# Layer 1: the low part of the row maxima made by TensorE and copied out by ScalarE

## The chip, the cores and the metric

The kernel runs on one core of one Trainium2 chip. The metric is the device time of one execution in microseconds (us). Three runs of the kernel before gave 2096.59, 2102.5 and 2103.61 us; the median is 2102.5 us.

## What is computed

The reference is two transformer layers over x of shape (64, 64, 256), each a cross attention and a mixture of experts:

```
x = x + L0_xattn(layernorm(x), ctx)        # 8 heads of 8 channels, 256 positions, rotary
x = x + L0_ffn(layernorm(x))               # 64 experts, 8 chosen, no capacity
x = x + L1_xattn(layernorm(x), ctx)        # as above, biases on q, k, v, no rotary, no output matrix
x = x + L1_ffn(layernorm(x))               # 64 experts, 8 chosen, capacity 128 each
```

In an attention, scores = q k / sqrt(8), p = softmax(scores), out = p v. For the change only one detail matters. The softmax subtracts the maximum of each row of scores. The kernel does this inside the product: q gets extra rows that hold minus the row maximum, and k has ones there. The products are in bf16, so the maximum is given in two bf16 rows, a high part (the maximum rounded to bf16) and a low part (what the rounding left).

## The kernel before, in words

Both layers have an attention stage and an expert stage, with barriers between them. The attention stage of a layer goes over 32 pairs of batches as a pipeline written out by hand. A pair passes the stages load, comb, front, stack, smax, attn, back, route, place and post, one stage in each step, so a step works on up to ten pairs at once. A step has 16 units u = 0..15. In each engine's program one function `body(st)` lists, unit by unit, what that engine does in the step; engines work their lists in order and meet only at semaphores.

Abbreviations used below, for unit u of a step:

- S(u): TensorE makes scores of the smax pair (line 1534) into one of three banks psS. VectorE then takes the row maxima from it (line 1145, "reduction"), negated, into mx. S(u) waits for the reduction of u-3.
- T(u): TensorE makes the transposed scores of the attn pair (line 1547), two matmuls, into one of two banks psE; ScalarE takes the exponential of it (line 943, "exp(u)"). T(u) waits for exp(u-2).
- values: TensorE multiplies four exponentials with v (line 1570, 16 matmul records) at u = 2 (for the pair in stage back), 7, 11 and 15.
- V: TensorE's product of the context with the value matrix (line 1618, recorded under 1585), at u = 4 in layer 1. Its bank is psO, and it waits until ScalarE has copied the attention output out of that bank at u = 3 (line 923, osb).
- RK: two small products for the routing ranks at u = 2 (line 1608); LIST: eight products for the token lists at u = 14 (line 1656), after ScalarE has copied out the router's logits at u = 13.

The row maxima of a pair come in two halves, h = 0 and h = 1. For each half the order of work is: TensorE transposes 16 columns of mx into a small bank (items mT1 at u = 1 for the attn pair, mT0 at u = 10 for the smax pair); ScalarE copies the bank to bf16, the high part mhi (`max_rows`, line 930); VectorE subtracts the high part from the bank, the low part mlo (`split_max`, line 1152), at u = 2 for h = 1 and at u = 11 for h = 0; the sync engine's queue writes both into rows of q2 (lines 674 and 706). T(0) waits for the half h = 0 of its pair, T(8) for h = 1. The small bank comes free for the next item when the low part is done (semaphore s_mlo).

In layer 1 ScalarE also multiplies gathered expert rows at u = 0..3 (line 950), normalises at u = 4 and 6 (lines 991 and 983), and TensorE's Q product at u = 7 waits for the second of these. POOL gathers those rows with eight indirect DMAs a step, paced by the exponentials.

Of the kernel before, what the change touches and what calls it, by code (L numbers as in the profile page):

```python
# [28 lines left out]
ALU = mybir.AluOpType  # L29
# [173 lines left out]
def build(nc, x, ctx, tables, wts, out):  # L203
    stack = ExitStack()
    with stack:
        def sb(name, shape, dt=F32):
            return stack.enter_context(nc.sbuf_tensor(name, shape, dt))

        def sem(name):
            return stack.enter_context(nc.semaphore(name))  # L210

        def sems(name, n=NB):
            return [sem(f"{name}{i}") for i in range(n)]
# [19 lines left out]

        ident = sb("ident", [P, P])
        ones = sb("ones", [P, P], BF16)
        tri = sb("tri", [P, P], BF16)
        tri0 = sb("tri0", [P, P], BF16)
        iota_e = sb("iota_e", [P, E])
# [148 lines left out]
        s_p1, s_rem, s_p2, s_p3 = (sem(n) for n in ("s_p1", "s_rem", "s_p2", "s_p3"))  # L387
        s_score, s_max = sem("s_score"), sem("s_max")
        s_mhi, s_mT, s_mlo = sems("s_mhi", 2), sems("s_mT", 2), sems("s_mlo", 2)
        s_st, s_exp = sem("s_st"), sem("s_exp")  # L390
        s_pv, s_oev = sem("s_pv"), sem("s_oev")
        s_vp, s_v = sem("s_vp"), sem("s_v")
# [514 lines left out]
        def _(act):  # L907
# [5 lines left out]
            def body(st):  # L913
# [11 lines left out]
                def max_rows(stage, h):  # L925
                    act.wait_ge(s_mT[h], st.n(stage))
                    before = Step(L, st.s0 - 1, st.it)
                    if before.s0 >= LAG[stage]:
                        act.wait_ge(d_max[h][before.buf(stage)], before.nbuf(stage, 32))
                    a.copy(mhi[h][:, :], small[item_bank(L, f"mT{h}")][0:16, 0:P]).then_inc(s_mhi[h], 1)  # L930

                filled = L == 1 and st.s0 == FULL - 2
                for u in range(UNITS):
                    if u == 15 and 0 <= st.s0 - AHEAD < EARLY // 2:
# [40 lines left out]
                        a.copy(xT[:, :, :].rearrange("p c t -> p (c t)"), small[item_bank(L, "XT")][:, 0:2 * P]).then_inc(s_xT, 1)  # L975
                    if u == 10 and st.on("smax"):
                        max_rows("smax", 0)
                    if u == (14 if filled else 4) and (st.on("front") or st.on("route")):
                        act.wait_ge(s_rstd, 4 * st.roots())
                    if u == (14 if filled else (4, 6)[L]) and st.on("front"):  # L980
# [79 lines left out]
        def _(dve):  # L1060
# [54 lines left out]
            for b in range(NB):  # L1115
                for o in range(2):
                    v_.memset(ones_of(b, o), 1.0)
            v_.tensor_copy(iota_e[:, :], iota_i[:, 0:E])
            v_.scalar_tensor_tensor(tri0[:, :], ident[:, :], CHOSEN, tri[:, :], ALU.mult, ALU.add)
            v_.tensor_copy(slotk[:, :], slot_i[:, :])  # L1120
            v_.tensor_copy(base0[:, :], base_i[:, :])
# [16 lines left out]
            def body(st):  # L1138
# [10 lines left out]
                def split_max(stage, h):  # L1149

                    dve.wait_ge(s_mhi[h], st.n(stage))
                    v_.tensor_tensor(mlo[h][:, :], small[item_bank(L, f"mT{h}")][0:16, 0:P], mhi[h][:, :], ALU.subtract)\
                      .then_inc(s_mlo[h], 1)
# [75 lines left out]
                for u in range(UNITS):  # L1229
# [21 lines left out]
                    if L == 1 and u == 9 and st.on("back"):  # L1251
# [3 lines left out]
                        wait(dve, d_x1[b], lastbuf(st, "back"))  # L1255
                        v_.scalar_tensor_tensor(x1[b][:, :], small[item_bank(1, "NT")][:, 0:T], bias[:, 8:9],
                                                xres[b][:, :], ALU.add, ALU.add).then_inc(s_x1, 1)
                    if u == 11 and st.on("smax") and not filled:
                        split_max("smax", 0)
                    if u == 1 and st.on("post") and L == 1:  # L1260
                        ch.join("ranks")
# [9 lines left out]
                    if L == 1 and st.s0 >= FULL - 1:  # L1271
                        sums(st, u)
                    if filled and u == 7:
                        split_max("smax", 0)
                        sums(Step(1, FULL - 3), 0)
                    if L == 1 and st.s0 < FULL - 1 and st.s0 != FULL - 3 and u == 15:
                        sums(st, 0)
# [29 lines left out]
                    if u == 0 and st.on("post") and L == 1:  # L1307
# [1 line left out]
                        wait(dve, s_lsp, st.n1("post", 1, 0))  # L1309
                        v_.tensor_tensor(twos(hotr[:, :, :]), over_k(rank_at), in_twos(0, P), ALU.is_equal)\  # L1310
                          .then_inc(s_lhs, 1)
                    if u == 2 and st.on("attn"):
                        split_max("attn", 1)
                    if L == 0 and u == 12 and st.on("back"):
                        b = st.buf("back")
# [205 lines left out]
        def _(pe):  # L1521
# [3 lines left out]
            def body(st):  # L1525
# [49 lines left out]
                def product(item, stage, ready, terms, done, n=T):  # L1575

                    for semaphore, value in ready:
                        pe.wait_ge(semaphore, value)
                    ps = psE[0] if item == "Q" and L == 1 and st.s0 == FULL - 2 else bank(pe, st, item)
                    for i, (lhs, rhs) in enumerate(terms):  # L1580
                        if rhs is None:
                            w = lhs.shape[1] if len(lhs.shape) == 2 else 32
                            ins = m_.transpose(ps[0:w, i * P:(i + 1) * P], lhs, ident[:, :])
                        else:
                            ins = m_.matmul(ps[:, i * n:(i + 1) * n], lhs, rhs, start=True, stop=True)
                    ins.then_inc(done, 1)

                def rows_of_x(st):
                    b = st.buf("route")
                    product("XT", "route", [(s_xr, st.n("route"))],  # L1590
                            [(xr[b][:, i * P:(i + 1) * P], None) for i in range(2)], s_xtp)

                def q_rows(st):
                    b = st.buf("front")
                    product("Q", "front", [(s_xn, st.n("front"))],
                            [(wbd[L][n][:, :], xn[b][:, :]) for n in ("qr", "q")[L]], s_qp)

                for u in range(UNITS):
# [2 lines left out]
                    if st.on("attn"):  # L1601
                        scores_t(u)
                    if u == 1 and st.on("attn"):
                        product("mT1", "attn", [(s_max, st.n("attn", UNITS))],
                                [(mx[st.buf("attn")][:, 1, :], None)], s_mT[1])
                    if u == 2 and st.on("place"):
                        b = st.buf("place")
                        product("RK", "place", [(s_mask, st.n("place"))],
# [26 lines left out]
                        product("NT", "back", [(s_nrm, st.n("back"))],  # L1635
                                [(nrm[:, h, :], None) for h in range(2)], s_ntp)
                    if u == 10 and st.on("smax"):
                        product("mT0", "smax", [(s_max, st.n("smax", UNITS, 8))],
                                [(mx[st.buf("smax")][:, 0, :], None)], s_mT[0])
                    if L == 0 and u == 10 and st.on("route"):  # L1640
                        rows_of_x(st)
                    if u == 12 and st.on("back") and L == 0:
# [137 lines left out]
```

## Time and profile before

| what | value |
|---|---|
| median of three runs | 2102.5 us |
| the profiled execution | 2111.01 us |
| its span (first to last instruction) | 2109.3 us |
| mean granted TensorE clock | 0.940 |
| busy share of the span: TensorE matmul, weight load | 79%, 52% |
| busy share: VectorE, ScalarE, GpSimd | 66%, 59%, 46% |

Matmuls overlap in TensorE's pipeline and their ends are modelled, so its busy share says little by itself. The page's list of costliest groups is headed by the reductions (681.1 us in 1024 instructions) and the exponentials (599.6 us in 1024, with 324.1 us of idle ScalarE time ahead of them, 263.2 us of it ended by a matmul of T). Those groups hold both layers. The attention stage of layer 1 is the stretch of some 675 us that ends with the reductions and exponentials at about 1844 us. In a timeline row the columns are: start in us, duration in us (of a merged row from its first start to its last end), engine, line, operation, output and inputs, size, count; in brackets the idle time of the engine before it and what ended that.

### The profile page before, as it was taken

Reading aid. Unit: us, or ns where it says so; the run is one execution under the profiler, and the core shown is the slowest. Engines: PE = TensorE matmul, PEld = TensorE weight load, DVE = VectorE, ACT = ScalarE, POOL = GpSimd, SP = SyncE. Lnnn points to the kernel's source line nnn. Section 1 sums busy time; section 2 is a strip of 40 time slices with the busy share of each in tenths; the row PEclk is TensorE's granted clock in tenths of the full one; section 3 lists DMA queues with packets and bytes.
Section 4 is the critical chain, followed back from the end, with each engine's and each line's share of the span. In section 5 each row is a group of like instructions: output and inputs, shape, how many; then the busy total and the mean of one; then the engine's idle time right before and its main releaser. Section 6 shows DMA issues by size and latency. Waiting matters only on the chain. (4 is left out here: it accounts for less than half of the span.)

```text
span 2109.3 us, 44138 instructions
## 1 busy us (share of the span) xinstructions
PE 1657.1 (79%) x12469; PEld 1104.4 (52%) x12623; DVE 1387.0 (66%) x4213; ACT 1238.4 (59%) x3174; POOL 978.2 (46%) x1114
## 2 busy tenths in 40 slices
PE   3999999999855999999994577777777778856651
PEld 2555555555534898899883244444444434444431
DVE  5888888888844455554334678878888778743331
ACT  1777777777642566666663467767777767722110
POOL 4277777777662000000004655555555553148883
PEclk9999999999987999999996799999999999968896
DMA  5688877777746966666664768877677676268856
GB/s 144 159 232 237 225 210 206 212 209 205 195 145 221 290 204 196 203 195 203 198 190 144 187 173 210 205 193 179 175 176 183 160 178 155 72 170 186 184 94 111
DMA packets 413082, 390.90 MB, mean 185 GB/s; under 512 B 46640, under 2 KB 385072, under 8 KB 412848
## 3 DMA queue, kind: packets, MB, share of 16 engines
q1 hardware_dynamic: 346496, 265.28, 47.1%
q0 software_dynamic: 37904, 90.22, 16.8%
q10 hardware_dynamic: 28448, 32.59, 5.5%
q8 instruction: 110, 1.80, 0.4%
q14 instruction: 124, 1.02, 0.2%
HBM read 233.74 MB, written 170.16 MB: 191 GB/s over the span
## 5 line engine op out<-in xcount | busy, mean ns | idle before, releaser
L1145 DVE TENSOR_REDUCE mx<-psS 128x2 f32<-128x512 f32 x1024 | 681.1, 682 | 176.9 <-PE psS L1534 113.4
L943 ACT ACTIVATE prob<-psE 128x512 f32<-128x512 f32 x1024 | 599.6, 600 | 324.1 <-PE psE L1547 263.2
L792 POOL DMA_INDIRECT yg<-y_d,row_all x256 | 252.4, 986 | 676.1 <-SPq L418 478.9
L1547 PE MATMUL psE<-q,k 128*128 128x256 bf16 x2048 | 397.3, 276 | 88.3 <-ACT prob L943 55.0
L1534 PE MATMUL psS<-k,q 128*128 128x512 bf16 x870 | 338.6, 390 | 27.3 <-DVE mx L1145 13.5
L1673 PE MATMUL psE<-wt,xgT 128*128 (+1 forms) x1536 | 327.2, 337 | 1.0 <-ACT xgT L1039 0.4
L779 POOL DMA_INDIRECT xs_d<-xr,row_all x256 | 252.0, 984 | 144.3 <-ACT prob L943 97.4
L1547 PEld LDWEIGHTS psE<-q,k 128*128 128x128 bf16 x2048 | 183.4, 99 | 254.6 <-ACT prob L943 119.0
L1486 DVE TENSOR_TENSOR hid<-sil,psE 128x96 f32<-128x96 f32 x384 | 97.7, 254 | 329.8 <-ACT sil L1044 307.0
L1570 PE MATMUL psO<-prob,v 128*32 128x256 f32 x4096 | 282.3, 394 | 0.0
L1039 ACT COPY xgT<-psS 128x256 f32<-128x256 f32 x384 | 144.5, 376 | 184.7 <-PE psS L1667 119.2
L1673 PEld LDWEIGHTS psE<-wt,xgT 128*128 128x128 f32 x1536 | 249.1, 196 | 6.3 <-issue 4.8
L1685 PE MATMUL psM<-wt,hT 96*128 (+1 forms) x768 | 235.1, 388 | 0.0
L1667 PE MATMUL psS<-ident,xg 128*128 128x128 f32 x768 | 155.0, 284 | 93.1 <-DMA xg<-xn_d,idx 82.0
L1667 PEld LDWEIGHTS psS<-ident,xg 128*128 128x128 f32 x768 | 105.0, 145 | 154.0 <-DMA xg<-xn_d,idx 87.0
L1534 PEld LDWEIGHTS psS<-k,q 128*128 128x128 bf16 x1024 | 103.1, 101 | 155.1 <-issue 76.0
L1048 ACT COPY y_all<-psM 128x256 f32<-128x256 f32 x320 | 119.2, 373 | 87.7 <-PE psM L1685 87.4
L1570 PEld LDWEIGHTS psO<-prob,v 128*32 128x32 f32 x4096 | 108.6, 111 | 96.7 <-issue 41.6
L1044 ACT ACTIVATE sil<-psE 128x96 f32<-128x96 f32 x384 | 96.6, 252 | 96.0 <-PE psE L1673 90.6
L1685 PEld LDWEIGHTS psM<-wt,hT 96*128 96x128 f32 x768 | 118.9, 195 | 15.5 <-issue 0.4
L838 POOL TENSOR_TENSOR parts<-rem,parts 128x512 bf16<-128x512 f32 x64 | 74.1, 1158 | 68.7 <-ACT parts L1017 33.3
L830 POOL TENSOR_TENSOR rem<-qk,parts 128x512 f32<-128x512 f32 x64 | 74.2, 1160 | 37.1 <-ACT parts L1008 22.9
(226 smaller groups left out, 2446.3 us busy)
## 6 DMA issues: line engine op xcount, KB each, us to landing
xg<-xs_d SPq DMA_DIRECT2D x320, 128.0 KB, 2.6
y_d<-y_all SPq DMA_DIRECT2D x320, 128.0 KB, 2.3
q<-q_stack_d SPq DMA_DIRECT2D x128, 256.0 KB
k<-k_stack_d SPq DMA_DIRECT2D x128, 256.0 KB
wt<-in_gu ACTq DMA_DIRECT2D x110, 192.0 KB
q_stack_d<-parts SPq DMA_DIRECT2D x64, 192.0 KB
k_stack_d<-parts SPq DMA_DIRECT2D x64, 192.0 KB
wt<-in_dn ACTq DMA_DIRECT2D x110, 96.0 KB
```

The costliest lines, as they stand in the source:

```text
L779: g.indirect_dma_start(xs_d[:, :], bass.IndirectOffsetOnAxis(row_all[:, row(st.pair(stage) * K + k, 1)], 0), xr[b][:, 0:T], None).then_inc ...
L792: g.indirect_dma_start(yg[:, k, :], None, y0_d[:, :], bass.IndirectOffsetOnAxis(row_all[:, row(st.pair("load") * K + k, 1)], 0))\
L943: a.activation(prob[gr][:, u % 4, :], psE[ring][:, :], ACT.Exp, scale=SCALE).then_inc(s_exp, 1)
L1039: a.copy(xgT[st.buf("X", 2)][:, :, :].rearrange("p c t -> p (c t)"), psS[st.buf("X", 2)][:, 0:2 * P]).then_inc(s_xgT, 1)
L1048: a.copy(y[st.buf("D")], psM[st.buf("D", 2)][:, 0:T]).then_inc(s_y, 1)
L1145: v_.tensor_reduce(mx[b][:, bg // 4, :].rearrange("p (h r) -> p h r", h=2)[:, :, (bg % 4) * 2 + tt], psS[(UNITS * (st.s0 - LAG["smax"]) + ...
L1534: m_.matmul(psS[(UNITS * (st.s0 - LAG["smax"]) + u) % 3][:, :], q2[b][:, bg, tt * P:(tt + 1) * P], k2[b][:, bg, :], start=True, stop=True) ...
L1547: ins = m_.matmul(psE[ring][:, i * T:(i + 1) * T], k2[b][:, bg, hh * T + i * P:hh * T + (i + 1) * P], q2[b][:, bg, :], start=True, stop=True)
L1570: ins = m_.matmul(psO[32 * j:32 * j + 32, half * T:(half + 1) * T], v[b][:, i, unit_at(4 * q + j), :], prob[gr][:, j, i * T:(i + 1) * T], ...
L1667: ins = m_.transpose(psS[i][:, c * P:(c + 1) * P], xg[b][:, c * P:(c + 1) * P], ident[:, :])
L1673: ins = m_.matmul(psE[i][:, 0:2 * I], xgT[i][:, c, :], weights_of(st, "GU", table, P, 2 * I * c, 2 * I), start=(c == 0), stop=(c == 1))
L1685: m_.matmul(psM[i][:, 0:T], hT[i][:, :], weights_of(st, "D", table, I, 4 * I, T), start=True, stop=True).then_inc(s_yp, 1)
```

## The change

In layer 1 VectorE no longer makes the low part; layer 0 keeps it. A new tile `minus` holds minus the identity, 16 by 16, in bf16. In layer 1 TensorE, one unit after the transposition (u = 2 for h = 1, u = 11 for h = 0), waits until the high part is made, and then writes the same 16 by 128 place of the small bank again with two matmuls: the maxima times the identity in f32, and, added to it, minus the identity times the high part. ScalarE copies the sum out as the low part at u = 3 (h = 1) and u = 12 (h = 0). The DMAs that carry the parts, and the semaphore that frees the bank, stay.

```
+        minus = sb("minus", [16, 16], BF16)
+        s_rest = sems("s_rest", 2)
 # ScalarE
+                def max_rest(stage, h):
+                    act.wait_ge(s_rest[h], st.n1(stage))
+                    a.copy(mlo[h][:, :], small[item_bank(L, f"mT{h}")][0:16, 0:P]).then_inc(s_mlo[h], 1)
...
+                    if L == 1 and u == 3 and st.on("attn"):
+                        max_rest("attn", 1)
+                    if L == 1 and u == 12 and st.on("smax"):
+                        max_rest("smax", 0)
 # VectorE
+            v_.tensor_scalar(minus[:, :], ident[0:16, 0:16], -1.0, None, ALU.mult)
...
-                    if u == 11 and st.on("smax") and not filled:
+                    if L == 0 and u == 11 and st.on("smax"):
                         split_max("smax", 0)
...
-                        split_max("smax", 0)
...
-                    if u == 2 and st.on("attn"):
+                    if L == 0 and u == 2 and st.on("attn"):
                         split_max("attn", 1)
 # TensorE
+                def less_high(stage, h):
+                    pe.wait_ge(s_mhi[h], st.n(stage))
+                    rest = small[item_bank(L, f"mT{h}")][0:16, 0:P]
+                    m_.matmul(rest, mx[st.buf(stage)][:, h, :], ident[:, :], start=True, stop=False)
+                    m_.matmul(rest, minus[:, :], mhi[h][:, :], start=False, stop=True).then_inc(s_rest[h], 1)
...
+                    if L == 1 and u == 2 and st.on("attn"):
+                        less_high("attn", 1)
...
+                    if L == 1 and u == 11 and st.on("smax"):
+                        less_high("smax", 0)
```

On TensorE the new pair at u = 2 stands after T(2) and before RK and the values of u = 2; at u = 11 it stands after T(11) and the values of u = 11, and before S(12). On ScalarE the new copy at u = 3 stands after exp(3), a product of the gathered rows and the copy osb, and before exp(4); at u = 12 after exp(12) and osb, and before exp(13).

## Rows read from the trace of the kernel before

**Rows 1.** Busy time and instructions by stretch; last: clock, DMA share, GB/s.

```profile
core 0: us, PE busy (x) PEld busy (x) DVE busy (x) ACT busy (x) POOL busy (x), PEclk, DMA share, GB/s
1169.00:1843.90 674.90, 517.26 (x4456) 283.03 (x4535) 555.12 (x1437) 477.93 (x1116) 354.15 (x428) 0.96 0.69 173
...
1506.50:1514.52 8.02, 6.00 (x51) 3.82 (x50) 7.28 (x20) 7.93 (x20) 3.85 (x4) 1.00 0.43 123
1514.52:1527.25 12.73, 9.54 (x91) 5.11 (x94) 10.26 (x30) 7.46 (x17) 7.05 (x10) 1.00 0.82 186
...
1502.50:1505.90 3.40, 3.40 (x28) 1.45 (x26) 1.73 (x9) 1.28 (x3) 2.54 (x5) 0.50 0.56 169
```

**Rows 2.** Groups by line and shape, 1250 to 1760: busy, mean ns, idle before.

```profile
L1152 DVE TENSOR_TENSOR mlo<-psM,mhi 16x128 bf16<-16x128 f32 x48 | 12.9, 269 | 0.8 <-ACT mhi L930 0.6 <-issue 0.2
...
L943 ACT ACTIVATE prob<-psE 128x512 f32<-128x512 f32 x385 | 228.4, 601 | 138.4 <-PE psE L1547 115.6 <-remote 18.5 <-PE psO L1570 2.4
...
L1585 PE MATMUL psO<-proj_v,ctx 128*128 128x128 f32 x96 | 16.4, 293 | 37.7 <-ACT osb L923 22.0 <-issue 15.7
```

**Rows 3.** Timeline of ScalarE in the first units of one step.

```profile
1506.50 0.60 ACT L943 ACTIVATE prob<-psE 128x512 f32<-128x512 f32 x1 [1.81 <-PE psE L1547]
...
1508.27 0.24 ACT L930 CAST mhi<-psM 16x128 bf16<-16x128 f32 x1
1508.41 0.58 ACT L943 ACTIVATE prob<-psE 128x512 f32<-128x512 f32 x1
...
1509.77 0.58 ACT L943 ACTIVATE prob<-psE 128x512 f32<-128x512 f32 x1
...
1510.65 0.36 ACT L923 COPY osb<-psO 128x256 f32<-128x256 f32 x1
1510.90 0.61 ACT L943 ACTIVATE prob<-psE 128x512 f32<-128x512 f32 x1
...
1512.31 0.60 ACT L943 ACTIVATE prob<-psE 128x512 f32<-128x512 f32 x1
```

**Rows 4.** Timeline of TensorE in the same units.

```profile
1507.15 0.39 PE L1547 MATMUL psE<-q,k 128*128 128x256 bf16 x2
1507.38 0.19 PE L1585 MATMUL psM<-mask,tri 128*128 128x64 bf16 x1
...
1508.76 0.38 PE L1547 MATMUL psE<-q,k 128*128 128x256 bf16 x2 [0.16 <-issue]
...
1511.15 0.68 PE L1585 MATMUL psO<-proj_v,ctx 128*128 128x128 f32 x4 [1.57 <-ACT osb L923]
1511.67 0.38 PE L1534 MATMUL psS<-k,q 128*128 128x512 bf16 x1
1511.89 0.38 PE L1547 MATMUL psE<-q,k 128*128 128x256 bf16 x2
```

**Rows 5.** Timeline of VectorE in the same units.

```profile
1509.02 0.27 DVE L1152 TENSOR_TENSOR mlo<-psM,mhi 16x128 bf16<-16x128 f32 x1
1509.22 0.67 DVE L1145 TENSOR_REDUCE mx<-psS 128x2 f32<-128x512 f32 x1
...
1512.09 0.69 DVE L1145 TENSOR_REDUCE mx<-psS 128x2 f32<-128x512 f32 x1 [0.74 <-PE psS L1534]
```

**Rows 6.** Timeline of TensorE from unit 11 to the next step.

```profile
1520.35 1.07 PE L1570 MATMUL psO<-prob,v 128*32 128x256 f32 x16
...
1524.63 0.61 PE L1657 MATMUL psM<-hote,hotr 128*128 128x128 bf16 x8 [0.57 <-ACT logit L1013]
1525.07 0.38 PE L1534 MATMUL psS<-k,q 128*128 128x512 bf16 x1
...
1526.83 0.38 PE L1547 MATMUL psE<-q,k 128*128 128x256 bf16 x2 [0.16 <-issue]
```

**Rows 7.** Timeline of ScalarE at units 10 and 12 of that step.

```profile
1521.42 0.24 ACT L930 CAST mhi<-psM 16x128 bf16<-16x128 f32 x1
...
1523.02 0.60 ACT L943 ACTIVATE prob<-psE 128x512 f32<-128x512 f32 x1 [0.87 <-PE psE L1547]
```

**Rows 8.** Timeline of the sync engine's queue in that step.

```profile
1523.10 0.54 SPq L706 DMA_DIRECT2D q<-mlo  x1
```

More of the change, by code:

```diff
@@ L1591, in rows_of_x, with max_columns @@
                             [(xr[b][:, i * P:(i + 1) * P], None) for i in range(2)], s_xtp)
+                def max_columns(stage, h, units):
+                    product(f"mT{h}", stage, [(s_max, st.n(stage, UNITS, units))], [(mx[st.buf(stage)][:, h, :], None)],
+                            s_mT[h])
+                def less_high(stage, h):
[3 more added lines that the diff above has]
+                    m_.matmul(rest, minus[:, :], mhi[h][:, :], start=False, stop=True).then_inc(s_rest[h], 1)
                 def q_rows(st):
@@ L1603, in body @@
                     if u == 1 and st.on("attn"):
-                        product("mT1", "attn", [(s_max, st.n("attn", UNITS))],
-                                [(mx[st.buf("attn")][:, 1, :], None)], s_mT[1])
+                        max_columns("attn", 1, UNITS)
+                    if L == 1 and u == 2 and st.on("attn"):
+                        less_high("attn", 1)
                     if u == 2 and st.on("place"):
@@ L1637, in body @@
                     if u == 10 and st.on("smax"):
-                        product("mT0", "smax", [(s_max, st.n("smax", UNITS, 8))],
-                                [(mx[st.buf("smax")][:, 0, :], None)], s_mT[0])
+                        max_columns("smax", 0, 8)
+                    if L == 1 and u == 11 and st.on("smax"):
+                        less_high("smax", 0)
                     if L == 0 and u == 10 and st.on("route"):
```

## The prediction

> **What bounds the kernel now.** The change touches only the attention stage of layer 1, so I read that stretch first and not the page's shares. By stretch, no engine is full over its 675 us: VectorE works 555 us, TensorE 517, ScalarE 478 [rows 1]. Such a stage is bound by a chain that runs from engine to engine, and the question is which engine holds it at the two places that change.
>
> The groups by line and shape tell how regular the stage is [rows 2]. In 510 us the low part is made 48 times, two a step, so there are 24 steps of about 21.2 us. Ahead of V TensorE was idle 37.7 us in 24 steps: 1.57 us each, ended by the copy osb, and the step that I follow has exactly 1.57 [rows 4]. So one step stands for the others.
>
> In that step the 8.02 us from exp(0) to the end of unit 6 have ScalarE busy 7.93 [rows 1]: up to there the chain runs on ScalarE. VectorE has 7.28 us in it and waits 0.74 us for S(5) [rows 5]. In the other 12.73 us ScalarE works only 7.46, and most of its 5.8 us of idle time a step (138.4 / 24) is ended by a T matmul [rows 1, 2]: there TensorE is late.
>
> So TensorE's position ahead of exp(3), and again ahead of exp(12), matters more than VectorE's work.
>
> **What is removed.** VectorE loses 0.269 us twice a step [rows 2]; from one start to the next it is 0.20 us [rows 5]. At u = 2 the next reduction would start 0.20 us earlier, but VectorE waits for S(5) two reductions later anyway, so this returns nothing. At u = 11 the reduction of u = 12 follows S(12), which, with T(12), stands behind the late values [rows 6, 7]. I take no gain; if VectorE did hold the chain it would be 64 x 0.20 = 12.8 us, and the few waits ahead of the subtraction (0.8 us) on top. That is one end of the range.
>
> **What is added at u = 2.** TensorE works in order, and now waits for the high part between T(2) and RK. T(2) starts at 1507.15 and RK at 1507.38 [rows 4]. The high part ends at 1508.27 + 0.24 = 1508.51, since ScalarE does it after exp(1) and a product of gathered rows [rows 3]. A release takes 0.05 us (exp(0) ends at 1507.10, T(2) starts at 1507.15). So the new pair starts at 1508.56.
>
> Its price is not in the trace. The nearest f32 matmul with 128 columns is V: two matmuls make four records, and from V to S(5) are 0.52 us, so one f32 matmul takes 0.26 [rows 4]. The bf16 one is bounded by LIST, eight of 128 columns in 0.44 us, 0.055 each [rows 6]. I take 0.32 together; the whole 0.68 us of V is the upper end, and 0.2 the lower.
>
> RK then starts at 1508.88, 1.50 us later. Queued behind are RK, the values of u = 2, S(3) and T(3). T(3) moves from 1508.76 to 1510.26. A T is ready for its exponential 0.42 us after its start (T(5) at 1511.89, exp(5) at 1512.31), so exp(3) starts at 1510.68 instead of 1509.77: 0.91 us late, because ScalarE was working on other things for the first 0.6 us of the delay.
>
> From exp(3) ScalarE keeps its own spacing: osb 0.88 us later (1511.56), the new copy at 1511.81, and exp(4) 0.14 us after that, the spacing of the high part's copy: 1511.95 instead of 1510.90, 1.05 late. V follows osb's end by 0.14 us, so it starts 0.91 us late, and with it S(5), T(5) and exp(5). ScalarE's own path to exp(5) has 1.05 at most. I take **0.91 us a step**; the cover of the new copy is V's wait, and without that cover it costs 0.14 more. VectorE's reductions from u = 3 on come as late, since S(3) stands behind the same wait. The work after unit 5 hangs on this chain (the second normalisation and Q), so nothing regular gives it back.
>
> **What is added at u = 11 and 12.** Here the pair stands behind the values of u = 11. The high part of this half ends at 1521.66 [rows 7], while the values start at 1520.35 and take 1.07 by the record [rows 6], and exp(12), which comes after them, starts at 1523.02 after 0.87 us of waiting for T(12). So the wait costs about nothing, but the pair's 0.32 us stand ahead of T(12), for which ScalarE waits: 0.32 on the path. The copy at u = 12 delays exp(13) and the logits by 0.14 us; LIST waits 0.57 us for the logits [rows 6], and S(15), T(15), the last values and the next T(0) stand behind LIST. So the 0.14 is on the path too: **0.46 us a step**. Lower end 0 (the late stretch swallows it), upper end 0.68 + 0.24.
>
> Of the moved copy the Trainium skill has a rule that speaks against it (ScalarE: Activation LUTs, Rules for kernel authors): multiplications, additions and the like belong on VectorE, which it gives as up to about three times faster. By that figure the copy would take an estimated 0.8 us, 0.57 more, and the sum would grow by 17 us in 30 steps. This trace does not agree for so small a tile: the copy of the same 16 by 128 takes 0.24 us on ScalarE [rows 3] and the subtraction 0.269 on VectorE [rows 2], and the sum goes by these.
>
> **The low part's way on.** The half h = 1 is written to q2 about 2 us later, long before T(8). The half h = 0 is needed by T(0) of the next step, at 1526.83 [rows 6]; the queue issued its low part at 1523.10 [rows 8]. It would be issued at about 1524.5, and T(0) itself comes 0.46 later, so some 2.8 us remain for a write of 4 KB. The issues queued behind it (x1 out, the next loads, the stack writes) move by up to 1.4 us, and what waits for them is over a unit away. I count nothing, and keep it as a rival. The small bank comes free later too, at u = 3 still ahead of K at u = 5, and K is behind V. The setup instruction and the new tile are single and cost nothing visible.
>
> **The sum.** 32 steps have the u = 2 pair; in the first the pipeline is still filling and I leave it out: 31 x 0.91 = 28.2 us. For u = 11 and 12 I count 30 of 32, since the last steps have no gathers and TensorE is less late: 30 x 0.46 = 13.8. Together 42.0 us on the profiled execution's 2111.0: 2153.0. The median of the runs is 8.5 us below that execution, so the forecast is 2102.5 + 42.0 = **2144.5 us**.
>
> **The rivals.**
>
> *A, the late stretch swallows the delay.* Between units 7 and 12 ScalarE waits for TensorE for longer than its recorded matmuls explain, in a stretch with a DMA share of 0.82 against 0.43 before it [rows 1]. If that ends by transfers that do not hang on the delayed chain, the 0.91 is lost in it, and 13.8 us stay: 2116.3; if it also swallows the pair of u = 11, nothing stays: 2102.5. Against it: those transfers are issued behind V, or paced by the exponentials, and so move with the chain.
>
> *B, VectorE holds the chain, and the kernel becomes faster.* VectorE is the busiest engine of the steps, 17.54 of 20.75 us [rows 1]. If TensorE's wait at u = 2 were covered by the 1.57 us that it waits ahead of V anyway, the relief of VectorE would count: 12.8 + 0.8 + some waits, about 15 us, 2087.5. It decides where exp(3) comes no later than now, that is where the delay of T(3) stays under 0.6 us instead of 1.50. Against it: the high part ends 1.36 us after T(2) starts, by two rows.
>
> *C, the clock.* After a pause TensorE's clock was granted at 0.50, the lower level of 1.2 GHz, from 1502.50 to 1505.90, and TensorE worked all of that time [rows 1]: at 2.4 GHz the same work takes half, so one such fall costs up to 1.70 us. The new wait makes another pause in each step. If each of the 23 regular steps fell once, 39 us come on top: 2183.5. Against it: the pause of 1.57 us ahead of V lies in a stretch granted at 1.00, and the new wait shortens it. The Trainium skill (TensorE: Matmul & The Clock Gate, HAM oscillation) says that waits between bursts of matmuls put the clock back to half; the trace agrees for the one fall shown, not for the pause ahead of V.
>
> *D, the low part lands late.* If its write takes 0.7 us longer than the 2.8 that remain, T(0) waits in 30 steps: 21 us more, 2165.5.
>
> **How the numbers follow.** Chances: forecast 0.60, A 0.15 (half of it at each of its two times), B 0.14, C 0.07, D 0.04. About 0.3%, 6 us, is what a measurement of this kernel can tell from no change. Faster by more: B, 0.14. Within: the lower half of A, 0.07. Slower: the rest, 0.79. The forecast's own range is 2125 to 2165, by the pair's price (0.2 to 0.68), the copy (0 to 0.14) and a partial loss in the late stretch. The range to hold eight times in ten adds A and D and leaves out B and C: 2100 to 2170.
>
> **What would show it.** Right: V's idle time falls from 1.57 to about 1.0 us and a new idle time of about 1 us stands ahead of the new pair at u = 2; exp(3) starts about 4.2 us after exp(0) instead of 3.27, exp(5) 6.7 instead of 5.81; the steps take about 22.5 us instead of 21.2. The prediction is wrong if exp(3) keeps its place, if steps keep their length although exp(5) comes late (A), if VectorE's reductions close up (B), or if the granted clock falls in most steps (C).

## The result, and the profile after

The changed kernel takes 2139.65 us (median of 4 runs, 2138.02 to 2145.36), the kernel before 2100.91 us in the runs beside them (4 runs, 2096.59 to 2103.61). The change is slower, by 38.7 us between the medians; the ratio is 1.0172, 95% interval 1.0149 to 1.0195, which is 36 us. The forecast was 2144.5 us. The profiled execution after took 2145.36 us (span 2143.7), 5.7 us over its median; that of before lay 10 us over its own. So a comparison of the two traces shows 34.35 us, some 4 us less than the medians.

By stretch (columns as in [rows 1]), first the whole attention stage of layer 1 after the change, then the two parts of one of its steps:

```profile
1169.00:1877.80 708.80, 551.78 (x4720) 293.13 (x4718) 544.67 (x1372) 489.28 (x1179) 352.67 (x428) 0.97 0.65 165
1545.95:1555.00 9.05, 6.70 (x55) 3.89 (x53) 6.81 (x17) 7.11 (x19) 4.50 (x6) 1.00 0.54 152
1555.00:1568.54 13.54, 10.28 (x97) 5.28 (x97) 10.56 (x30) 8.65 (x19) 7.35 (x10) 1.00 0.72 174
```

The stage ends at 1877.8 instead of 1843.9, so 33.9 of the 34.35 us are in it. VectorE has 65 instructions fewer and works 10.4 us less, which buys nothing. The granted clock is 0.97 against 0.96 [rows 1]: it did not fall more often.

The groups by line and shape after the change, over 24 steps from 1254.5 to 1790.8 (busy us, mean ns of one, idle us ahead of it, and what ended that), the counterpart of [rows 2]:

```profile
L949 ACT ACTIVATE prob<-psE 128x512 f32<-128x512 f32 x385 | 226.1, 593 | 153.7 <-PE psE L1557 133.9 <-remote 13.6 <-issue 5.7
...
L1612 PE MATMUL psM<-ident,mx 128*16 128x128 f32 x96 | 18.9, 278 | 29.8 <-ACT mhi L932 24.1 <-issue 5.6
...
L1595 PE MATMUL psO<-proj_v,ctx 128*128 128x128 f32 x96 | 16.4, 293 | 30.7 <-ACT osb L925 30.7
...
L936 ACT CAST mlo<-psM 16x128 bf16<-16x128 f32 x48 | 12.0, 250 | 0.0
...
L1613 PE MATMUL psM<-mhi,minus 16*16 16x128 bf16 x48 | 10.5, 218 | 0.0
```

The new copy (L936) takes 250 ns, and ScalarE has no idle time ahead of it. The new pair (L1612, L1613) stands at u = 2 behind 24.1 us of waiting for the high part, 1.00 us a step; the other 5.6 us, to which the profile gives no cause, stand ahead of the pair at u = 11. V (L1595) waits 30.7 / 24 = 1.28 us a step instead of 1.57. ScalarE's wait for its exponentials grew by 15.3 us, by more T matmuls that come late.

TensorE in one step, u = 2 to 5 (start, duration, what it is; in brackets the idle time ahead and what ended it), the counterpart of [rows 4]; exp(0) starts at 1545.95:

```profile
1546.60 0.39 PE L1557 MATMUL psE<-q,k 128*128 128x256 bf16 x2
...
1548.01 0.39 PE L1612 MATMUL psM<-ident,mx 128*16 128x128 f32 x2 [1.01 <-ACT mhi L932]
1548.33 0.22 PE L1613 MATMUL psM<-mhi,minus 16*16 16x128 bf16 x1
1548.48 0.20 PE L1595 MATMUL psM<-mask,tri 128*128 128x64 bf16 x1
...
1549.87 0.38 PE L1557 MATMUL psE<-q,k 128*128 128x256 bf16 x2
...
1552.03 0.68 PE L1595 MATMUL psO<-proj_v,ctx 128*128 128x128 f32 x4 [1.34 <-ACT osb L925]
...
1552.76 0.38 PE L1557 MATMUL psE<-q,k 128*128 128x256 bf16 x2
```

ScalarE in the same units, the counterpart of [rows 3]:

```profile
1545.95 0.60 ACT L949 ACTIVATE prob<-psE 128x512 f32<-128x512 f32 x1 [0.94 <-PE psE L1557]
...
1547.72 0.24 ACT L932 CAST mhi<-psM 16x128 bf16<-16x128 f32 x1
...
1550.63 0.60 ACT L949 ACTIVATE prob<-psE 128x512 f32<-128x512 f32 x1 [1.31 <-PE psE L1557]
...
1551.52 0.36 ACT L925 COPY osb<-psO 128x256 f32<-128x256 f32 x1
1551.77 0.25 ACT L936 CAST mlo<-psM 16x128 bf16<-16x128 f32 x1
1551.93 0.58 ACT L949 ACTIVATE prob<-psE 128x512 f32<-128x512 f32 x1
...
1553.18 0.60 ACT L949 ACTIVATE prob<-psE 128x512 f32<-128x512 f32 x1
```

The pair starts 2.06 us after exp(0), where the prediction had it (1508.56 - 1506.50). RK follows 0.47 us later, not 0.32. From RK to T(3) are 1.39 us, as before (1.38). But exp(3) starts 0.76 us after T(3), not 0.42: T(3)'s result came 0.34 us late too.

One step can mislead, so I worked out the same from all starts of exp(u) in the 23 steps in the middle of the stage, each with its eight gathers (mean start after exp(0), us):

```
             exp3  exp4  exp5  exp6  exp7  exp8  exp11 exp12 exp13 step
before       3.27  4.40  5.81  7.05 10.09 11.73 14.63 16.76 17.51 21.32
after        4.62  5.92  7.17  8.64 10.57 12.97 15.86 17.87 18.78 22.40
difference  +1.35 +1.52 +1.36 +1.59  +.48 +1.24 +1.23 +1.11 +1.27 +1.08
```

exp(3) lies between 4.34 and 4.85 in these steps. Up to exp(5) every step agrees with the mean to within 0.3 us. The steps themselves do not: they take 20.0 to 24.8 us before and 20.8 to 25.9 after, so a difference in the right half of the table is uncertain by some 0.2 to 0.4 us. As far as that allows, the loss is made at u = 2, and what comes after adds nothing that stays.

### The profile page after: what moved, and what is told of

It reads as the page before. It is cut to its first block and busy times, and to the rows that moved or that the text cites. A ratio compares the mean times of both kernels' runs of the same rounds, so it can differ in the third digit from the quotient of the medians.

```text
span 2143.7 us, 44677 instructions
## 1 busy us (share of the span) xinstructions
PE 1700.5 (79%) x12815; PEld 1114.3 (52%) x12815; DVE 1378.4 (64%) x4150; ACT 1249.4 (58%) x3238; POOL 976.8 (46%) x1114
## 3 DMA queue, kind: packets, MB, share of 16 engines
q14 instruction: 124, 1.02, 0.2%
## 5 line engine op out<-in xcount | busy, mean ns | idle before, releaser
L1544 PE MATMUL psS<-k,q 128*128 128x512 bf16 x1024 | 397.7, 390 | 21.0 <-DMA k<-k_stack_d 12.0
L1595 PE MATMUL psM<-xn,proj_q 128*128 128x256 f32 x126 | 45.2, 442 | 60.5 <-ACT xn L993 44.6
```

The costliest lines, as they stand in the source:

```text
L1544: m_.matmul(psS[(UNITS * (st.s0 - LAG["smax"]) + u) % 3][:, :], q2[b][:, bg, tt * P:(tt + 1) * P], k2[b][:, bg, :], start=True, stop=True) ...
```

## The experiments

A gain or loss in us is the ratio's distance from 1 times the median of the kernel before, run beside it; the change's own is 36 us by this count.

**The wait or the work at u = 2?** The first takes the kernel before and lets TensorE wait at u = 2 as the changed one does, with no pair. The second has the pair without the wait.

```diff
+                    if L == 1 and u == 2 and st.on("attn"):
+                        pe.wait_ge(s_mhi[1], st.n("attn"))
                     if u == 2 and st.on("place"):
```

> The kernel before, with one wait more: TensorE waits at u = 2 for the high part of the half h = 1, between T(2) and RK, and does nothing with it; VectorE keeps the subtraction. Theory (the wait in TensorE's order is what costs): T(3) comes 1.18 us later, exp(3) 0.59 us later or more, so the time is some 31 x 0.6 to 31 x 0.9 = 18 to 28 us above the kernel before. Rival (the two matmuls and the copy cost, the wait is covered by TensorE's 1.57 us ahead of V): within 5 us of the kernel before.

2113.78 us against 2102.08: 1.006 (1.0037 to 1.0083), 13 us. The timeline of TensorE at u = 2 (RK), and then of ScalarE (exp(0) and exp(3)), of this kernel:

```profile
1511.99 0.20 PE L1585 MATMUL psM<-mask,tri 128*128 128x64 bf16 x1 [1.02 <-ACT mhi L930]
```

```profile
1509.93 0.60 ACT L943 ACTIVATE prob<-psE 128x512 f32<-128x512 f32 x1 [0.94 <-PE psE L1547]
...
1513.80 0.60 ACT L943 ACTIVATE prob<-psE 128x512 f32<-128x512 f32 x1 [0.50 <-PE psE L1547]
```

exp(3) is at 3.87, 0.60 late in every regular step, as worked out. The 13 us are fewer than the 18 that were expected at the least: 0.4 of the 0.6 us a step stay. In the profiled execution exp(11) is still 0.60 late and exp(12) 0.15, and the step has its old length (21.29 us), but this trace lies 2 us under its median and that of before 10 us over, some 0.4 us a step between them. So a part of the delay is taken back, between units 11 and 12 by this trace; how much of it, and by what, the two traces do not settle.

```diff
+        minus = sb("minus", [16, 16], BF16)
...
+            v_.tensor_scalar(minus[:, :], ident[0:16, 0:16], -1.0, None, ALU.mult)
...
                     if u == 2 and st.on("place"):
                         b = st.buf("place")
+                        if L == 1 and st.on("attn"):
+                            pe.wait_ge(s_mask, st.n("place"))
+                            ps = bank(pe, st, "RK")[0:16, 0:P]
+                            m_.matmul(ps, mx[st.buf("attn")][:, 1, :], ident[:, :], start=True, stop=False)
+                            m_.matmul(ps, minus[:, :], ones[0:16, :], start=False, stop=True)
```

> The kernel before, with two matmuls more at u = 2 of layer 1 that wait for no high part: the maxima times the identity in f32 and minus the identity times a bf16 tile of ones, written into the place of RK just before RK overwrites it; 28 steps have them. VectorE keeps the subtraction. Theory (the wait costs, not the work): T(3) comes 0.47 us later, which exp(3) does not feel because ScalarE is still busy for 0.6 us: within 5 us of the kernel before. Rival (TensorE's time at u = 2 is on the path): 28 x 0.47 = 13 us slower.

2107.18 us against 2102.08, 1.0019 (1.0007 to 1.0031): 4 us, by the bound of 0.3% no change. exp(3) stays at 3.27.

**Both together, without the copy on ScalarE.** The second experiment with the wait ahead of the pair; VectorE keeps its subtraction.

```diff
+                            pe.wait_ge(s_mhi[1], st.n("attn"))
                             pe.wait_ge(s_mask, st.n("place"))
                             ps = bank(pe, st, "RK")[0:16, 0:P]
```

> The kernel before, with the wait for the high part and two matmuls of the pair's size at u = 2 (written into the place of RK before RK overwrites it); VectorE keeps the subtraction, ScalarE has no copy. Together with the wait alone (+12.6 us) and the half h = 1 alone (+36 us) it splits the 36 us. Theory: the pair behind the wait is all on the path, so 12.6 + 28 x 0.47 or more, where the gathers' transfers then make T(3) late: 28 to 36 us above the kernel before, exp(3) at 4.34 or later. Rival (the copy on ScalarE costs): 12 to 20 us above.

2143.44 us against 2110.65: 1.0167 (1.0137 to 1.0197), 35 us. exp(3) is at 4.60. So wait and pair at this one place make nearly the whole loss; the copy that moved to ScalarE, and the pair at u = 11, are not needed for it. They do not add: 13 and 4 us alone, 35 together. Much of that is one piece of slack: T(3) can be 0.6 us late before exp(3) is, since ScalarE is busy that long. The pair alone stays inside it, the wait alone uses it up, and then every further delay counts: exp(3) is 0, 0.60 and 1.33 us late in the three kernels.

**One half at a time.** From the changed kernel, one half goes back to VectorE.

```diff
-                    if L == 1 and u == 3 and st.on("attn"):
-                        max_rest("attn", 1)
...
-                    if L == 0 and u == 2 and st.on("attn"):
+                    if u == 2 and st.on("attn"):
                         split_max("attn", 1)
...
-                    if L == 1 and u == 2 and st.on("attn"):
-                        less_high("attn", 1)
```

> Only the half h = 0 is changed (pair at u = 11, copy at u = 12); the half h = 1 stays with VectorE. The prediction's term for this place is 30 x 0.46 = 14 us slower. Rival (TensorE's late stretch between units 7 and 12 swallows the pair, only the copy's 0.14 us remain): about 4 us slower, exp(12) as long after exp(11) as in the kernel before.

2112.51 us against 2102.08, 1.0047 (1.003 to 1.0063): 10 us, between the two expectations.

```diff
-                    if L == 1 and u == 12 and st.on("smax"):
-                        max_rest("smax", 0)
...
-                    if L == 0 and u == 11 and st.on("smax"):
+                    if u == 11 and st.on("smax") and not filled:
                         split_max("smax", 0)
...
+                        split_max("smax", 0)
...
-                    if L == 1 and u == 11 and st.on("smax"):
-                        less_high("smax", 0)
```

> Only the half h = 1 is changed (wait and pair at u = 2, copy at u = 3); the half h = 0 stays with VectorE. The prediction's term is 31 x 0.91 = 28 us slower. The trace of the changed kernel has the pair at 0.47 us and T(3)'s result late in most steps, exp(5) 1.31 us late on average: by that up to 31 x 1.31 = 41 us, less what the later units give back, 34 to 38 us. If it is near 34 and the half h = 0 alone near 4, the two add up to the whole change.

2139.88 us against 2102.08, 1.0171 (1.0151 to 1.0191), 36 us, the loss of the whole change to within 1 us. The half at u = 11 costs 10 us where the step is otherwise on time, and nothing on top of the late one (by the two intervals 0, give or take 6 us). Where these 10 us lie I could not see: only some 2 of them are in the last four steps, which have no gathers, and the other steps differ by less than one execution differs from the next.

**The same work two units later.** From the changed kernel, the pair moves from u = 2 to u = 4, just ahead of V, and its copy from u = 3 to 4.

```diff
-                    if L == 1 and u == 3 and st.on("attn"):
+                    if L == 1 and u == 4 and st.on("attn"):
                         max_rest("attn", 1)
...
-                    if L == 1 and u == 2 and st.on("attn"):
+                    if L == 1 and u == 4 and st.on("attn"):
                         less_high("attn", 1)
```

> The changed kernel, with the pair of the half h = 1 moved on TensorE from u = 2 to u = 4 (behind T(4), ahead of V, where TensorE waits 1.57 us for osb anyway) and its copy on ScalarE from u = 3 to u = 4 (behind exp(4)). Same work, no wait ahead of exp(3). Theory (place and wait cost): exp(3) is back at 3.27 us after exp(0), exp(5) at most 0.14 late, and the time is that of the change of the half h = 0 alone, 2112 us, or up to 4 us more. Rival (the work itself costs): stays near 2138.

2120.65 us against 2110.65, 1.0054 (1.0033 to 1.0075): 11 us instead of 36, about what the half at u = 11 costs alone. TensorE at u = 4 and 5:

```profile
1542.37 0.38 PE L1557 MATMUL psE<-q,k 128*128 128x256 bf16 x2
1542.68 0.39 PE L1612 MATMUL psM<-ident,mx 128*16 128x128 f32 x2
1543.01 0.22 PE L1613 MATMUL psM<-mhi,minus 16*16 16x128 bf16 x1
1544.33 0.68 PE L1595 MATMUL psO<-proj_v,ctx 128*128 128x128 f32 x4 [1.10 <-ACT osb L925]
```

No bracket stands at the pair: the high part has long been there, and the pair is done inside the idle time ahead of V, which falls from 1.57 to 1.10 us. exp(3) and exp(5) keep 3.27 and 5.81. At u = 2 the place cost the time, not the instructions.

**What takes the delay back in the late stretch?** Its DMA share and the gathers of expert rows made the transfers suspect. In both kernels each gather is replaced by a small transfer that no index steers, which leaves out the combination of the expert rows.

```diff
-                    g.indirect_dma_start(yg[:, k, :], None, y0_d[:, :],
-                                         bass.IndirectOffsetOnAxis(row_all[:, row(st.pair("load") * K + k, 1)], 0))\
-                     .then_inc(d_yg[k // 4], 16)
+                    g.dma_start(yg[:, k, 0:16], y0_d[row(0), 0:16]).then_inc(d_yg[k // 4], 16)
...
+                            if st.s0 == LAG["comb"]:
+                                act.wait_ge(s_clear, 2)
...
+                v_.memset(yg[:, :, 16:T], 0.0)
```

> The kernel before, with each of the eight indirect gathers a step replaced by a direct load of 16 elements a partition on the same queue: the combination of the expert rows of layer 0 is left out. Theory (TensorE's late stretch between units 7 and 12 comes with the gathers' transfers): ScalarE's idle time ahead of exp(7), exp(8) and exp(12) shrinks by 2 to 3 us a step, and the steps take 18 to 19 us, as the last step before the gathers end does (18.57). Rival (the late stretch comes from the stack loads or the matmuls themselves): steps stay above 20.5 us.

2043.86 us against 2110.65, 0.9682 (0.9656 to 0.9708).

> The changed kernel with the same replacement of the gathers; the combination is left out. Theory (the late stretch swallowed the pair of u = 11, and the gathers made TensorE late in unit 3): exp(3) at 4.34 in every step, exp(12) 0.4 us later against exp(11) than in the kernel before without gathers, and the two kernels without gathers differ by 1.08 + 0.4 + 0.14 = 1.6 us a step, some 50 us, more than the 38 with gathers. Rival (nothing is swallowed): they differ by 38 us or less.

2080.27 us, 0.986 (0.9833 to 0.9887). The change costs 36.4 us here (between the two medians), about what it costs with the gathers; the rival was right in the total. But it is now wholly regular: exp(3) is at 4.34 in every step, so its spread up to 4.85 came from the gathers. ScalarE at units 11 to 13 of one step, with exp(11) first, of the kernel before and then of the changed one, both without gathers:

```profile
1504.47 1.06 ACT L941 ACTIVATE prob<-psE 128x512 f32<-128x512 f32 x2
1506.48 0.60 ACT L941 ACTIVATE prob<-psE 128x512 f32<-128x512 f32 x1 [0.70 <-PE psE L1548]
```

```profile
1503.69 0.58 ACT L947 ACTIVATE prob<-psE 128x512 f32<-128x512 f32 x1
1504.95 0.60 ACT L947 ACTIVATE prob<-psE 128x512 f32<-128x512 f32 x1 [0.68 <-PE psE L1558]
1505.86 0.58 ACT L947 ACTIVATE prob<-psE 128x512 f32<-128x512 f32 x1
```

In the first, exp(11) and exp(12) run on end, 0.49 us from start to start, and exp(13) waits 0.70 us. In the second it is exp(12) that waits, 1.26 us after exp(11), and exp(13) follows at once. Up to exp(13) the pair of u = 11 costs 2.17 - 2.01 = 0.16 us only. This step is 1.02 us longer (0.95 on the mean of the 23): the 1.07 of u = 2 and nothing for u = 11. With the gathers exp(12) is late anyway: 2.13 us after exp(11) before the change.

**Bytes or form?** The same bytes on the same queue, but with rows in order that the address names directly, so the choice of the rows is left out:

```diff
-                    g.indirect_dma_start(yg[:, k, :], None, y0_d[:, :],
-                                         bass.IndirectOffsetOnAxis(row_all[:, row(st.pair("load") * K + k, 1)], 0))\
-                     .then_inc(d_yg[k // 4], 16)
+                    g.dma_start(yg[:, k, :], y0_d[row(st.pair("load") * K + k), :]).then_inc(d_yg[k // 4], 16)
```

> The kernel before, with each indirect gather replaced by a direct load of as many bytes (128 rows of 1 KB in order) on the same queue; the choice of the rows is left out. Theory (the bytes make TensorE late): steps stay near 21.3 us, time within 15 us of the kernel before. Rival (it is the indirect form): steps near 18.8 us, as with the small direct loads, some 65 us faster.

2042.63 us against 2111.44: 0.9687 (0.9663 to 0.971), as fast as without the bytes. The 24 steps by stretch (columns as in [rows 1]), of the kernel before and then of this one, and the group of the exponentials in this one:

```profile
1253.92:1763.96 510.04, 388.58 (x3390) 214.83 (x3448) 423.60 (x1125) 365.87 (x863) 286.89 (x339) 0.98 0.73 183
```

```profile
1246.52:1697.60 451.08, 372.92 (x3390) 213.46 (x3448) 440.14 (x1122) 364.82 (x863) 194.68 (x337) 1.00 0.81 207
```

```profile
L941 ACT ACTIVATE prob<-psE 128x512 f32<-128x512 f32 x384 | 224.0, 596 | 78.3 <-PE psE L1545 76.9
```

ScalarE's waits fall from 138.4 us [rows 2] to 78.3, and the same instructions of TensorE take 15.7 us less (at a granted clock of 1.00 instead of 0.98), while the DMA share rises from 0.73 to 0.81. My theory, the bytes, is wrong: the price hangs on the indirect form. Three things go with that form: the steering by an index, GpSimd's work on each gather (its busy time falls from 286.89 to 194.68 us) and rows that do not lie in order. No run tells them apart.

**Packed or spread.** In the kernel before, the gathers of a step are started by unit: 2, 3, 4, 5, 6, 7, 8, 9. Here they start earlier, and then spread.

```diff
-PACE = ((6, 8, 10, 12, 14, 0, 2, 4), (2, 3, 4, 5, 6, 7, 8, 9))
+PACE = ((6, 8, 10, 12, 14, 0, 2, 4), (0, 0, 0, 1, 2, 3, 4, 5))
```

> The kernel before, with the gathers of layer 1 paced by earlier exponentials: units 0, 0, 0, 1, 2, 3, 4, 5 instead of 2 to 9. They still wait for the products and additions that free their rows. Theory (gather traffic makes TensorE late, and costs only where TensorE holds the chain, from unit 7 on): more of the traffic falls into units 0 to 6, where ScalarE holds the chain with 0.6 us to spare ahead of exp(3), so the idle time ahead of exp(7) and exp(8) falls by 0.5 to 1 us a step: 15 to 25 us faster than the kernel before. Rival (the late gathers are held by the additions, and the early ones make T(3) and T(5) late): within 10 us of the kernel before, or slower.

2165.91 us, 1.0255 (1.0228 to 1.0281): the theory is wrong. The timelines of GpSimd, TensorE, ScalarE and VectorE in one step of this kernel, T(6) and exp(6) in the second and third:

```profile
1546.39 0.95 POOL L792 DMA_INDIRECT yg<-y_d,row_all  x1 [0.30 <-issue]
1547.64 0.95 POOL L792 DMA_INDIRECT yg<-y_d,row_all  x1 [0.31 <-issue]
1548.90 0.95 POOL L792 DMA_INDIRECT yg<-y_d,row_all  x1 [0.30 <-issue]
```

```profile
1547.31 0.38 PE L1547 MATMUL psE<-q,k 128*128 128x256 bf16 x2
```

```profile
1550.34 0.60 ACT L943 ACTIVATE prob<-psE 128x512 f32<-128x512 f32 x1 [2.48 <-remote]
```

```profile
1551.11 0.36 DVE L1158 RECIPROCAL rec<-psM 128x32 f32<-128x32 f32 x1 [2.23 <-remote]
```

The gathers run back to back, 1.26 us apart, and T(6) reaches its exponential 3.03 us after its start instead of 0.42. ScalarE stands ready and waits 2.48 us, ended by what the profile calls remote and shows nowhere. In the program exp(6) waits for T(6) alone, so it is T(6)'s result that comes late; VectorE waits 2.23 us in the same way for a later result of TensorE. The gathers did not leave the late stretch; they took the lateness with them, and the step grew to 23.36 us. So the opposite was tried: the same eight gathers with two of them moved to the end of the step. They stand behind GpSimd's remainder operations there. With all eight ahead of these and paced by units 2, 4, 6, 8, 10, 12, 13 and 14 the program would come to a standstill: ScalarE waits for a remainder operation, which stands behind gathers that wait for later exponentials of ScalarE.

```diff
+PACE = ((6, 8, 10, 12, 14, 0, 2, 4), (2, 4, 5, 7, 8, 9, 13, 14))
...
-                        for k in range(K):
+                        for k in range(6):
                             gather(st, k, PACE[L][k])
...
                     remainder()
                     third_part()
+                    if st.s0 >= FULL:
+                        for k in range(6, K):
+                            gather(st, k, PACE[L][k])
```

> The kernel before, with the eight indirect gathers of layer 1 spread over the step: units 2, 4, 5, 7, 8, 9, and the last two at 13 and 14, behind the two remainder operations of POOL. Theory (several indirect gathers close behind each other make TensorE late for some 3 us; with the early pacing the late stretch came right after the fifth of them): spread out, the late stretch becomes shorter or falls into gaps that are there anyway, 10 to 40 us faster than the kernel before. Rival (each gather costs TensorE its share wherever it lies, or the last ones come too late for the next step's additions): the same or slower.

2070.95 us against 2104.31: 0.984 (0.9819 to 0.986), 34 us faster than the kernel before. The exponentials over 24 steps, and the stretch, in this kernel:

```profile
L946 ACT ACTIVATE prob<-psE 128x512 f32<-128x512 f32 x384 | 227.4, 599 | 99.8 <-PE psE L1550 94.5 <-PE psO L1573 2.1 <-issue 1.4
```

```profile
1250.93:1725.09 474.16, 386.19 (x3454) 213.26 (x3451) 423.72 (x1126) 367.95 (x863) 280.71 (x338) 1.00 0.77 197
```

The same transfers, the same work of every engine, and ScalarE waits 38.6 us less than in [rows 2]; the step is 19.82 us. The wait ahead of exp(7) is gone (0.06 us on the mean). With fewer waits left, the change itself was tried once more, in its harmless place (pair and copy at u = 4) and with these gathers.

```diff
-PACE = ((6, 8, 10, 12, 14, 0, 2, 4), (2, 3, 4, 5, 6, 7, 8, 9))
+PACE = ((6, 8, 10, 12, 14, 0, 2, 4), (2, 4, 5, 7, 8, 9, 13, 14))
...
-                        for k in range(K):
+                        for k in range(6):
                             gather(st, k, PACE[L][k])
...
+                    if st.s0 >= FULL:
+                        for k in range(6, K):
+                            gather(st, k, PACE[L][k])
...
-                    if L == 1 and u == 3 and st.on("attn"):
+                    if L == 1 and u == 4 and st.on("attn"):
                         max_rest("attn", 1)
...
-                    if L == 1 and u == 2 and st.on("attn"):
+                    if L == 1 and u == 4 and st.on("attn"):
                         less_high("attn", 1)
```

> Both halves changed, the pair of h = 1 at u = 4 as in the kernel of that name, and the gathers spread as in the kernel before this one (2, 4, 5, 7, 8, 9, 13, 14). It asks whether VectorE's 0.40 us a step are worth anything once TensorE's late stretch is short. Theory (VectorE does not hold the chain; the pair of u = 11 and the copy of u = 12 do cost): 4 to 14 us slower than the spread gathers alone, a ratio of 0.986 to 0.991 to the kernel before. Rival (with the late stretch gone VectorE is the bound): faster than the spread gathers alone, a ratio below 0.982.

2099.42 us against 2115.28: 0.9921 (0.9894 to 0.9948). Slower than the spread gathers alone (0.984) by 17 us, just beyond what was expected: even here no gain from VectorE's relief is to be seen. The traces of the two tell where it is lost (mean start after exp(0) over the 23 steps, us):

```
               exp3  exp5  exp11 exp12 exp13 step
spread         3.30  5.83  13.58 15.06 15.81 19.82
and the change 3.32  5.85  13.59 15.38 16.31 20.63
```

Up to exp(11) the pair at u = 4 costs nothing. Then exp(12) is 0.32 us late, exp(13) 0.50 and the step 0.81 (uncertain by 0.2): here the half at u = 11 costs its full price. The best of the kernels that compute the whole is the one before with its gathers spread.

## Why the prediction came out, step by step

*VectorE's loss of two subtractions returns nothing: right.* With the subtractions kept on VectorE, the wait and the pair alone cost as much as the change (35 us); with them removed and the pair where it harms nothing at u = 2, no gain appears. Rival B is out: in no step with gathers did exp(3) keep its place.

*The wait at u = 2: right.* The pair starts 2.06 us after exp(0), as worked out, and 1.00 us a step is waited for the high part ("about 1"). V's wait went to 1.28 us, a little over the 1.0 forecast.

*The pair's price: too small.* 0.47 us to the next matmul, 0.15 over the 0.32 taken, inside the bounds. Without gathers exp(3) comes 1.07 us late in every step: the 0.91 of the prediction and these 0.15. With gathers it is 1.35 on the mean. The delayed T(3) now meets the first gather, which starts 3.26 us after exp(0), and its result is late as well. That went unseen in the prediction, which knew the slow stretch only from unit 7 on. So the term of 0.91 measured **1.36 us a step** at exp(5); 1.08, uncertain by 0.4, reach the step's end. By the run with this half alone, 36 us stand where 28.2 were forecast.

*The cover of the copy: right.* The copy makes exp(4) later by 0.17 us more than exp(3), but exp(5) only as late as exp(3): it goes by V, and V starts 0.51 us after osb starts, as before (0.50 in [rows 3, 4]).

*u = 11 and 12, 0.46 us a step: the step that failed.* It said of the pair that it stands "ahead of T(12), for which ScalarE waits", and of the copy that "the 0.14 is on the path too". On top of the late first half it came to nothing: 36 us with and without it, where 13.8 were forecast. From exp(11) to the end of the step it is 6.69 us before and 6.54 after, uncertain by 0.3. Here is TensorE before, S(12) of the step of [rows 6], and then the changed kernel in the step shown above, TensorE and ScalarE, the counterpart of [rows 6, 7]:

```profile
1521.36 0.39 PE L1534 MATMUL psS<-k,q 128*128 128x512 bf16 x1
```

```profile
1561.38 1.07 PE L1580 MATMUL psO<-prob,v 128*32 128x256 f32 x16
...
1562.73 0.39 PE L1612 MATMUL psM<-ident,mx 128*16 128x128 f32 x2 [0.28 <-issue]
...
1563.20 0.39 PE L1544 MATMUL psS<-k,q 128*128 128x512 bf16 x1
1563.43 0.38 PE L1557 MATMUL psE<-q,k 128*128 128x256 bf16 x2
```

```profile
1562.44 0.24 ACT L932 CAST mhi<-psM 16x128 bf16<-16x128 f32 x1
...
1564.20 0.60 ACT L949 ACTIVATE prob<-psE 128x512 f32<-128x512 f32 x1 [1.03 <-PE psE L1557]
...
1564.95 0.25 ACT L936 CAST mlo<-psM 16x128 bf16<-16x128 f32 x1
1565.11 0.58 ACT L949 ACTIVATE prob<-psE 128x512 f32<-128x512 f32 x1
```

Two things were wrong. The first is local: the prediction said that "the wait costs about nothing". The profile calls the 0.28 us ahead of the pair "issue", but the high part ends at 1562.68 and the pair starts 0.05 us later, the time of a release, and so it is in 22 of the 23 steps. The prediction's own rows had the high part end 0.24 us after the values. With the pair's 0.47 us S(12) starts 1.82 us after the values instead of 1.01, so 0.81 us late and not 0.32. The copy puts 0.16 us between exp(12) and exp(13), as forecast. The second is what becomes of it: a wait for a T matmul ahead of exp(12) does not mean that more work ahead of it prolongs it by as much. Under the gathers as they were the wait hangs on something else as well (what, was not shown), and where they are gone the next wait, ahead of exp(13), takes the delay up. With the gathers spread, though, the 0.81 us stay. In two of the last steps of the stage, the second and third from its end, which have no gathers, the terms stand nearly as written: +0.86 at exp(5), +0.43 from exp(11) to exp(12), +0.16 to exp(13), 1.53 us for the step. This is what rival A said of the pair of u = 11; what it said of the delay of u = 2 failed, since that was not lost in the late stretch.

*Clock and late low part: right to leave out.* The granted clock of the stage was 0.97, not below the 0.96 of before, and no T(0) came later by itself: the difference is 1.27 us at exp(13) and 1.08 at the next exp(0).

*The sum.* 42.0 us were forecast on the profiled execution and 34.35 came: 23 steps of 1.08 make 24.8, the four steps after them 6.0, the last step 1.0, the start and the steps before them the rest. That the time fits so closely is in part luck: one term was too small (28.2 for 36), another did not stay (13.8 for nothing), and the errors have opposite signs.

What stays open: how much of a delay of 0.6 us the late stretch takes back and why it does not do so with 1.3, and where the 10 us of the half at u = 11 lie when it is changed alone.

## What to carry to other kernels

Before work is moved to an engine that works in order, find what its first wait will be and what is queued behind it: the same pair cost 25 us less two units later, where its operand had come and the engine was idle anyway. An idle time ended by an engine is no proof that more work on that engine prolongs it; take the suspected other cause away (here the gathers) and look whether the wait goes. An idle time that the profile calls "issue" may still be a wait: compare its end with the end of what the program waits for there. And delays do not add: 13 and 4 us alone were 35 together, because both draw on the same slack once, and 10 and 36 alone were 36.

## What the runs showed of the hardware

In these runs, indirect gathers that follow each other closely hold up results that do not depend on them. The profile names TensorE or nothing as the cause, since T is recorded at its usual place and only its exponential starts late: in the step shown 3.03 us after T(6) with packed gathers, where a T that is on time is ready after 0.42. The bytes are not the reason: direct transfers of the same bytes, at a higher DMA share, bring the kernel to 0.9687, the same as almost no bytes (0.9682), which puts the price of the indirect form, with GpSimd's work on it and rows out of order, at some 66 us. How it comes about was not shown; that spacing helps (0.984) and packing harms (1.0255) was. The other number is small: 16 by 128 values leave the accumulation buffer in 0.250 us by ScalarE's copy and took 0.269 by VectorE's subtraction [rows 2], so neither engine was the cheaper place. The figure for which the prediction names a page (the Trainium skill, ScalarE: Activation LUTs, Rules for kernel authors) is given there for bf16 and operations with one source; this subtraction has two sources, one of them f32, so the prediction's estimate of 0.8 us for the copy does not follow from it.
